# A decoder kernel's first cross attention: batches in turn, scores in three fp32r passes, splits and shares on POOL

## What is computed

```python
kv_rope = kv_c * cos[None] + _rotate_half(kv_c) * sin[None]
q_r = jnp.einsum('bshq,hqr->bhsr', q_big, W_qr)
k_r = jnp.einsum('bld,hdr->bhlr', kv_rope, W_kr)
scores = jnp.einsum('bhsr,bhlr->bhsl', q_r, k_r)
attn = jax.nn.softmax(scores, axis=-1)
ctx_c = jnp.einsum('bhsl,bld->bhsd', attn, kv_rope)
ctx_lat = jnp.einsum('bhsd,hkd->bshk', ctx_c, w_kc_kv)
out = ctx_lat.reshape(b, s, H * K) @ Wo.T
```

## Time and profile before

| | us |
|---|---|
| median of 3 runs (lowest, highest) | 1678.25 (1677.41, 1680.61) |
| the profiled execution: its time | 1680.23 |
| its span in the profile | 1678.4 |
| busy in it: PE, DVE | 1602.4, 991.4 |
| busy in it: ACT, POOL | 730.2, 508.6 |
| busy from 436 to 642 us (the stage): PE | 199.63 |
| DVE, ACT, POOL there | 146.00, 142.43, 5.47 |

### The profile page before, as it was taken

How to read it: one execution, slowest core, us unless ns; L and a number is a source line. 1 busy time by engine, 2 the same in 40 slices (tenths; PEclk the granted TensorE clock), 3 DMA queues, 4 the chain that set the end, 5 groups by cost and what they waited for, 6 DMA issues and landing times.

```text
span 1678.4 us, 24116 instructions
## 1 busy us (share of the span) xinstructions
PE 1602.4 (95%) x9668; PEld 1329.3 (79%) x9668; DVE 991.4 (59%) x1658; ACT 730.2 (44%) x1221; POOL 508.6 (30%) x335
## 2 busy tenths in 40 slices
PE   7999999999899999989999989999889999999998
PEld 6897667778688888867889987787677888878887
DVE  5555663455676675487758748244757455554555
ACT  2113664223577765666611146422635334353442
POOL 3875542520100002331117734111611432212321
PEclk9999999999999999999999999999999999999999
DMA  4110003134312004410001110110001111111111
GB/s 164 53 61 28 2 2 130 39 99 130 106 53 64 13 1 161 156 38 1 1 1 63 50 39 1 44 43 32 21 14 44 51 53 55 51 45 51 51 57 44
DMA packets 28578, 88.49 MB, mean 53 GB/s; under 512 B 4154, under 2 KB 4282, under 8 KB 28215
## 3 DMA queue, kind: packets, MB, share of 16 engines
q1 hardware_dynamic: 28468, 86.96, 15.6%
HBM read 85.11 MB, written 1.84 MB: 52 GB/s over the span
## 4 chain that ended last, share of the span: by engine, by line
PE 85%; DVE 8%; ACT 4%; issue 1%; POOL 0%; DMA 0%; ACTq 0%; DVEq 0%
PE PS L255 18%; PE PS L257 17%; PE PS L256 17%; PE PS L260 6%; PE PS L1026 5%; PE PS L1044 4%; PE PS L1376 3%; PE PS L932 3%; PE PS L1391 2%; PE PS L542 2%; PE PS L566 1%; PE PS L1623 1%; PE PS L1611 1%; PE PS L532 1%; DVE sm L1645 1%
## 5 line engine op out<-in xcount | busy, mean ns | idle before, releaser
L301 POOL TENSOR_TENSOR HL<-stg,HL 128x1024 fp32r<-128x1024 f32 (+2 forms) x111 | 244.0, 2201 | 824.2 <-ACT HL L296 803.8
L255 PE MATMUL PS<-XT,HL 128*128 128x448 f32 x608 | 225.3, 371 | 7.5 <-DVE XT L336 5.3
L257 PE MATMUL PS<-XT,HL 128*128 128x448 f32 x608 | 223.5, 368 | 0.0
L256 PE MATMUL PS<-XT,HL 128*128 128x448 f32 x608 | 223.5, 368 | 0.0
L296 ACT ACTIVATE HL<-stg 128x1024 fp32r<-128x1024 f32 (+2 forms) x111 | 104.2, 943 | 217.8 <-PE PS L257 202.5
L255 PE MATMUL PS<-HL,XT 128*128 128x512 f32 (+1 forms) x380 | 138.6, 365 | 3.7 <-DVE rs L316 1.6
L257 PE MATMUL PS<-HL,XT 128*128 128x512 f32 (+1 forms) x380 | 135.4, 356 | 0.0
L256 PE MATMUL PS<-HL,XT 128*128 128x512 f32 (+1 forms) x380 | 135.3, 356 | 0.0
L255 PEld LDWEIGHTS PS<-XT,HL 128*128 128x128 f32 x608 | 115.0, 189 | 19.1 <-DVE XT L336 6.0
L256 PEld LDWEIGHTS PS<-XT,HL 128*128 128x128 f32 x608 | 115.0, 189 | 9.7
L257 PEld LDWEIGHTS PS<-XT,HL 128*128 128x128 f32 x608 | 114.9, 189 | 9.8
(11 more groups left out here) (283 smaller groups left out, 3603.2 us busy)
## 6 DMA issues: line engine op xcount, KB each, us to landing
stg<-in_wst SPq DMA_DIRECT2D x87, 512.0 KB, 3.5
stg<-in_wst SPq DMA_DIRECT2D x16, 352.0 KB, 3.1
stg<-in_wst SPq DMA_DIRECT2D x16, 320.0 KB, 3.8
wsum<-in_wfc SPq DMA_DIRECT2D x8, 512.0 KB, 4.1
wsum<-in_wpj SPq DMA_DIRECT2D x8, 512.0 KB, 3.6
raw<-in_wfc SPq DMA_DIRECT2D x8, 512.0 KB, 6.7
stg<-in_wst SPq DMA_DIRECT2D x16, 256.0 KB, 2.6
raw<-in_wpj SPq DMA_DIRECT2D x7, 512.0 KB, 7.0
```

Source lines behind the costliest of these rows:

```text
L255: e.matmul(out, lh, rh, start=start, stop=False)
L256: e.matmul(out, lh, rl, start=False, stop=False)
L257: return e.matmul(out, ll, rh, start=False, stop=stop)
L301: e.tensor_tensor(slot(k)[:, 1, 0:n], stg[k % NSTG][:, 0:n], slot(k)[:, 0, 0:n].bitcast(F), A.subtract).then_inc(*done("pool_w", k))
```

## The change

- **Order.** Unit st takes batch `st // 8`: all 16 heads of a batch, then the next batch. `qx_at` and `pair_of` use slots 0 to 15 of `QO` (results go where the queries were); the freed slot and the room behind it hold the split queries.
- **Scores.** `mm3` on split queries (`qxh`, `qxl`: four heads of a batch, two buffers) and split keys (`kxh`, `kxl`: one batch, two buffers, padded by one column to 376).
- **POOL.** A new stage `pool_x` splits queries every second unit and the keys of the next batch every eighth, and scales the exponentials to shares, which DVE no longer does. The rest of "ox" 2 moves from the end of `pool_q` to step 3 of `pool_x`, behind the shares of unit 2.
- **Waits of PE.** It begins with the queries, the first split queries and the keys of batch 0, and waits for the last rotated values only ahead of the value products.
- **Hand-over.** Heads 0 to 7 are complete only at the end. `ox_hi` and `ox_lo` of the first four outputs are made in two parts: batches 0 to 5 in steps 52 to 59, batches 6 and 7 at the end of `act_x` and `dve_x` (there behind `threshold`). Tiles 0 to 4 of the first product need the first part alone.

```diff
+        kxh = [at(f"kxh{i}", [128, L + 1], R, (KVX + 6080, KVX)[i]) for i in range(2)]
...
         def qx_at(half, h):
-            s = 1 + 8 * (h // 8) + 4 * half
+            s = 8 * (h // 8) + 4 * half
             return QO[:, s:s + 4, h % 8, :]
...
             for b in range(NB):
                 rotate_rows(e, b)
-            for i in range(3):
...
+            last.then_inc(*done("pool_x", "pad"))
+            keys_parts(e, 0)
+            query_parts(e, 0)
+            for i in range(2):
                 rest_w(e, piece["ox", i][0])
...
+        def keys_parts(e, b):
+            e.wait_ge(*upon("dve_ctx", "k", b if b == 0 else NB - 1))
+            if b > 1:
+                e.wait_ge(*upon("pe_x", "sc", 8 * b - 9))
+            e.tensor_copy(kxh[b % 2][:, 0:L], kvT[:, b, :]).then_inc(*done("pool_x", "kh", b))
+            e.wait_ge(*upon("pool_x", "kh", b))
+            e.tensor_tensor(kxl[b % 2][:, 0:L], kvT[:, b, :], kxh[b % 2][:, 0:L].bitcast(F), A.subtract).then_inc(*done("pool_x", "k", b))
...
+        def query_parts(e, u):
+            i = u // 2 % 2
+            q = QO[:, 8 * (u // 4 % 2) + u // 8, 4 * i:4 * i + 4, :]
...
+            if u > 3:
+                e.wait_ge(*upon("pe_x", "sc", u - 3))
+            e.tensor_copy(qxh[i][:, :, :], q).then_inc(*done("pool_x", "qh", u))
+            e.wait_ge(*upon("pool_x", "qh", u))
+            e.tensor_tensor(qxl[i][:, :, :], q, qxh[i][:, :, :].bitcast(F), A.subtract).then_inc(*done("pool_x", "q", u))
+
+        def pool_x(e):
+            for st in range(UX + 1):
+                if st % 2 == 0 and st + 2 < UX:
+                    query_parts(e, st + 2)
+                if st % 8 == 4 and st // 8 + 1 < NB:
+                    keys_parts(e, st // 8 + 1)
+                if st:
+                    u = st - 1
+                    k = u % 4
+                    e.wait_ge(*upon("dve_x", "rx", u))
+                    for e_ in range(2):
+                        last = e.tensor_scalar(Sx[k][:, e_, :], Sx[k][:, e_, :], rx[:, k, e_:e_ + 1], None, A.mult)
+                    last.then_inc(*done("pool_x", "p", u))
+                if st == 3:
+                    rest_w(e, piece["ox", 2][0])
+
         def pe_x(e):
-            e.wait_ge(*upon("dve_q", "o", 7, 1))
-            e.wait_ge(*upon("act_q", "o", 7, 1))
-            e.wait_ge(*upon("dve_ctx", "k", 7))
-            e.wait_ge(*upon("pool_ctx", "k", 7))
             for st in range(UX + 4):
                 if st < UX:
-                    b, bank = st // 4 % 8, 2 * (st % 2)
-                    if st > 1:
+                    b, bank = st // 8, 2 * (st % 2)
+                    if st % 8 == 0:
+                        e.wait_ge(*upon("pool_x", "k", b))
+                    e.wait_ge(*upon("pool_x", "q", st // 2 * 2))
...
                     for e_ in range(2):
-                        last = e.matmul(PS[0:S, bank + e_, 0:L], QO[:, 1 + st // 4, 2 * (st % 4) + e_, :], kvT[:, b, :],
-                                        start=True, stop=True)
+                        i, j = st // 2 % 2, 2 * (st % 2) + e_
+                        last = mm3(e, PS[0:S, bank + e_, 0:L + 1], qxh[i][:, j, :], qxl[i][:, j, :], kxh[b % 2][:, :],
+                                   kxl[b % 2][:, :], True, True)
...
-                    e.wait_ge(*upon("dve_x", "p", u))
+                    e.wait_ge(*upon("pool_x", "p", u))
...
             value_hi(e, 1)
+            for c in range(4):
+                ox_hi(e, c, 1)
...
-                    e.wait_ge(*upon("dve_x", "rx", u))
-                    for e_ in range(2):
-                        last = e.tensor_scalar(Sx[k][:, e_, :], Sx[k][:, e_, :], rx[:, k, e_:e_ + 1], None, A.mult)
-                    last.then_inc(*done("dve_x", "p", u))
...
             threshold(e)
+            for c in range(4):
+                ox_lo(e, c, 1)
...
                 for t in range(NT):
+                    if c == 0 and t == 5:
+                        e.wait_ge(*upon("dve_ox", "lo", 0, 1))
```

More of the change, by code:

```diff
@@ L168, in build @@
         Sx = [at(f"Sx{i}", [S, 2, L], F, rSCR + i * 3008) for i in range(4)]
+        QOX, KVX = rQO + 16 * 8 * S * 4, rKV + 24288
+        qxh = [at(f"qxh{i}", [128, 4, S], R, QOX + i * 3584) for i in range(2)]
+        qxl = [at(f"qxl{i}", [128, 4, S], R, QOX + i * 3584 + 1792) for i in range(2)]
+        kxh = [at(f"kxh{i}", [128, L + 1], R, (KVX + 6080, KVX)[i]) for i in range(2)]
+        kxl = [at(f"kxl{i}", [128, L + 1], R, (KVX + 3008, KVX + 1504)[i]) for i in range(2)]
         PX = [at(f"PX{i}", [125, 2, 3, S], F, rSCR + 12032 + i * 2688) for i in range(2)]
@@ L1007, in pool_q @@
                 rotate_rows(e, b)
-            for i in range(3):
+            for i in range(2):
+                e.tensor_scalar(kxh[i][:, L:L + 1], C("ones")[:, 0:1], 0.0, None, A.mult)
+                last = e.tensor_scalar(kxl[i][:, L:L + 1], C("ones")[:, 0:1], 0.0, None, A.mult)
+            last.then_inc(*done("pool_x", "pad"))
+            keys_parts(e, 0)
+            query_parts(e, 0)
+            for i in range(2):
                 rest_w(e, piece["ox", i][0])
         UX = 64
+        def keys_parts(e, b):
[5 more added lines that the diff above has]
+            e.tensor_tensor(kxl[b % 2][:, 0:L], kvT[:, b, :], kxh[b % 2][:, 0:L].bitcast(F), A.subtract).then_inc(*done("pool_x", "k", b))
@@ new lines, in pair_of @@
+        def pair_of(u):
+            return QO[:, 8 * (u // 4 % 2) + u // 8, 2 * (u % 4):2 * (u % 4) + 2, :]
+        def query_parts(e, u):
+            i = u // 2 % 2
+            q = QO[:, 8 * (u // 4 % 2) + u // 8, 4 * i:4 * i + 4, :]
+            if u < 8 or u == 32:
+                e.wait_ge(*upon("dve_q", "o", u + 1 if u < 8 else 7, u // 32))
+                e.wait_ge(*upon("act_q", "o", u + 1 if u < 8 else 7, u // 32))
+            if u > 3:
[3 more added lines that the diff above has]
+            e.tensor_tensor(qxl[i][:, :, :], q, qxh[i][:, :, :].bitcast(F), A.subtract).then_inc(*done("pool_x", "q", u))
@@ L1042, in pe_x @@
                         e.wait_ge(*upon("dve_x", "o", u - 2))
+                    else:
+                        e.wait_ge(*upon("pool_ctx", "k", NB - 1))
                     for c in range(3):
-                        last = e.matmul(PS[:, 6 + u % 2, 0:2 * S], kvr[:, c, u // 4 % 8, :], PX[u % 2][:, :, c, :],
+                        last = e.matmul(PS[:, 6 + u % 2, 0:2 * S], kvr[:, c, u // 8, :], PX[u % 2][:, :, c, :],
                                         start=c == 0, stop=c == 2)
@@ L1112, in dve_x, with ox_batches, ox_src, ox_part @@
             threshold(e)
+            for c in range(4):
+                ox_lo(e, c, 1)
         OX = 16
         first_ox = piece["ox", 0][0]
[L1119 to L1126, removed]
+        def ox_batches(c, part):
+            return (0, NB) if c > 3 else (6 * part, 6 + 2 * part)
+        def ox_src(c, part):
+            b0, b1 = ox_batches(c, part)
+            return QO[:, 8 * (c // 8) + b0:8 * (c // 8) + b1, c % 8, :]
+        def ox_part(hl, c, part):
+            b0, b1 = ox_batches(c, part)
+            return XT[:, hl, c % 4, :].rearrange("p (b s) -> p b s", b=NB)[:, b0:b1, :]
+        def ox_hi(e, c, part=1):
+            e.wait_ge(*upon("dve_x", "o", 8 * ox_batches(c, part)[1] - 1))
             if c > 3:
                 e.wait_ge(*upon("pe_ox", "c", c - 4))
-            else:
+            elif part == 0:
                 e.wait_ge(*upon("act_mag", 15))
[L1131 to L1135, removed]
+            e.activation(ox_part(0, c, part), ox_src(c, part), ACT.Copy).then_inc(*done("act_ox", "hi", c, part))
+        def ox_lo(e, c, part=1):
+            e.wait_ge(*upon("act_ox", "hi", c, part))
+            e.tensor_tensor(ox_part(1, c, part), ox_src(c, part), ox_part(0, c, part).bitcast(F),
+                            A.subtract).then_inc(*done("dve_ox", "lo", c, part))
         def value_bank(j):
@@ L2368, in sync @@
             load(e, first_ox + 9)
[L2369 removed]
+            e.wait_ge(*upon("dve_ox", "lo", 7, 1))
             for j in range(7):
@@ L2404, in gpsimd @@
         def gpsimd(e):
-            for stage in (pool_proj0, pool_att0, pool_o0, pool_q, pool_ox, pool_ffn, pool_proj1, pool_att1, pool_o1, pool_q2, pool_att2,
+            for stage in (pool_proj0, pool_att0, pool_o0, pool_q, pool_x, pool_ox, pool_ffn, pool_proj1, pool_att1, pool_o1, pool_q2, pool_att2,
                           pool_o2, pool_moe):
```

18 lines of the change are left out of this document (10 added, 8 removed).

## The result

The changed kernel took 1715.7 us (median of 4 runs, 1711.91 to 1719.22), the kernel before 1679.43 beside it: ratio 1.0214, 95% interval 1.0199 to 1.0229. It is slower by 36 us, 2.1%; I had forecast 1672.6, faster. The profiled execution has a span of 1715.0 us against 1678.4.

A forecast was written before the change was run, and what follows sets the result against it. The prediction took PE to bound the stage, with POOL hidden: -13.6 us for the scores and +8.0 for a stall at the start gave -5.6, so 1672.6 us from a median of 1678.25, range 1662 to 1679.

The forecast's parts named there:

- the price of the scaling: POOL in the first cross attention: 0.55 us per scaling of 375 columns, from one-input rows.
- so POOL is hidden: POOL's work sums to 17.1 us per eight units, 2.1 a unit, against PE's 2.83.
- the upper bound: POOL's scalings and casts: at most the two-input price, 0.97 us per scaling.
- rival (b): POOL becomes the bound at two-input prices: 3.34 us a unit, 1702.8 us, slower; 10%.
- Scores: PE's scores in six fp32r matmuls at 0.172 us: unit 2.83, saving 13.6 us over 59 units.
- Rival (c): PE's weight loads are not hidden in the scores: +0.41 us a unit, 1710 us; 3%.
- The wait that takes its place: Stage start: late third weight rest delays the first wsum load, stalling ACT and PE; +8.0 us (+6 to +10.5).
- The gain of the earlier start: Stage start: batch order lets PE score before the last key rotation; -1.4 us if nothing stalled.
- Rival (a): The start does not stall, so PE gains 1.4 us there: 1663.3 us; 10%.
- The hand-over: Stage end: split output parts on DVE and ACT stay covered; 0 us, up to +2 if not.
- My terms: Whole kernel: -13.6 for the scores and +8.0 for the start, together -5.6 us.
- Moving the shares off DVE: DVE loses 0.74 us of work a unit, off the path: worth nothing.

The follow-up runs named there:

- e10: e2 with a second multiplication by 1.0 added to each POOL scaling; 1664.3 us.
- e2: The changed kernel with only the third weight rest ("ox" 2) moved back to the end of the queries' stage; 1703.2 us.
- e5: e2 with a constant as the scale in place of the reciprocal read from memory, so the division by the sums is left out; 1694.1 us.
- e3: The changed kernel with the scaling back on DVE and the third weight rest back in its early place; 1664.5 us.
- e4: e2 with one tensor_tensor of 112x750 and broadcast reciprocals on POOL in place of two tensor_scalar; 1664.8 us.
- e7: e4 with only the scores back to fp32 on unsplit queries and keys; 1681.2 us.
- e12: The changed kernel with only the second multiplication by 1.0 in the POOL scaling, third weight rest still late; 1674.0 us.
- e9: e2 with minimum and maximum with constants in place of the multiplication on POOL, division by the sums left out; 1665.3 us.

## Why the prediction was wrong

**The step that failed** is the price of the scaling, "I take 0.55", in the part on shares and splits, and with it "so POOL is hidden". The two rows of one-input operations behind it are both of instructions with two operations, a minimum and a maximum; the one-column row beside them, too, has two, both multiplications. I allowed for a scale read from memory; I did not note that the change's instruction has one operation where they all have two. That form takes 1.24 us, above even what I had set as the upper bound, the two-input price of 0.97. With it POOL needs, by the groups shown first, 16 x 1.24 for the shares, 4 x 1.69 for the queries and 1.42 for the keys, 28.0 us per eight units or 3.5 a unit, where PE needs 2.82. e10, with the second operation and nothing else changed against e2, brings it back to 0.596 us and the unit to 2.822.

**The rival (b) is what happened** (I had given it 10%): POOL became the bound. Its price was too low, though, and its reason another one: it took the two-input price as the dearest case and named the scale in memory, which e5 shows to be 0.08 us, not the single operation. Its figures were 3.34 us a unit and 1702.8; measured were 3.429 and 1715.7. Of the 12.9 us between, 5.1 are in the units (21.6 against 16.5), 2.0 in the start, 0.6 in the hand-over, and most of the rest is the scatter of the other stages. The low clock in mid-stage isn't among the causes, since POOL's work alone comes to the 3.5 us a unit.

**Scores: right.** Six matmuls at 0.172 were forecast to make the unit 2.83; it is 2.822 in e3, e4 and e10. e7 puts a price on that alone, 1681.2 against 1664.8, 16 us by medians and 13.6 by 58 x 0.235. The formula of the Trainium skill (TensorE: Matmul & The Clock Gate, Back-to-back issue gap), N/2.4 + 2.5 ns, gives 0.159 us for 376 columns, and by that estimate the unit would have been 2.75; it is 2.822, and the rows decided rightly. Rival (c), weight loads not hidden, is out: one score matmul follows the other at 0.17 us (three starts in a row at full clock are 657.47, 657.64 and 657.82).

**The wait that takes its place: right in mechanism, and in size once the scaling has the priced value.** e12 is the kernel I priced: start 26.05 against 19.02 before, +7.0 where +8.0 was forecast, and 1674.0 us where 1672.6 was forecast. Half of that 1.0 is the load, 4.0 us from its issue to the sum instead of 4.5. Behind unit 5's scores another 0.8 us is lost while the clock is still low (0.69 from 457 to 460 us). The gain of the earlier start, forecast as 1.4 if nothing stalled, is 19.02 - 17.41 = 1.6. In the change itself the start cost +10.0. Rival (a) fails with it.

**The hand-over: right.** From the scores of unit 63 to the first output product it is 11.1 us in every kernel where POOL doesn't bind, 11.14 before. DVE ended the four split parts near 680.2 us in the change, and no wait of PE for them shows.

**Sum.** My terms come to -5.6 and e12 measures 0.9966 of the kernel before, which is -5.7 us (-3.9 to -7.6 by its interval; the medians alone give -7.6). Term by term it is +7.0 and -12.8 against +8.0 and -13.6, so the agreement to 0.1 is in part two small errors that cancel. The large error was one price, 0.69 us too low in 128 instructions, and it turned some 6 us faster into 36 us slower.

## What to carry to other kernels

A price taken from another row must be of the same form of instruction: operation count, where the scalars come from, kinds of input. Moving the shares off DVE was counted as worth nothing in the prediction, and e3 and e4, level with each other, bear that out: it brought the risk and none of the gain. When a piece of work moves to an engine whose trace doesn't show it, work out from which price the engine binds, and treat a price with no row of its form as open in both directions, not as bounded by a dearer kind. And follow the queue of the transfer engine past every wait that the change moves: the rest of one weight piece held up sixteen loads that had nothing to do with it.

The best kernels here are the change with the third rest early and either form of cheap shares: e3, e4 and e10, 1664.3 to 1664.8 us, 0.99 of the kernel before. Among them the runs tell no difference; e10 is two small edits away from the change.

## What the runs showed that I had not expected

- POOL's tensor_scalar over 112 x 375 fp32 takes 1.24 us with one multiplication and 0.60 us with that and a second one by 1.0. With constants it is 1.17 for one operation and 0.50 for two (minimum and maximum). Why the form with one operation is slow no run here shows; width, alignment and the place of the scale are excluded.
- The scale's place in memory costs 0.08 us an instruction (e5 against e2). The 0.10 between e9 and e10 has that and another pair of operations in it.
- A multiplication of two inputs, one of them broadcast, on 750 columns takes 1.44 us, less than one of 375 columns twice in the slow form (2.49).
- DVE's scalings are slower where POOL casts queries at the same time: in e3 two of them take 1.04 us instead of 0.74.
- PE was busy for 87% of the stretch from 475 to 640 us (143.26 of 165), and its granted clock still fell in places. Around the wait of 2.20 us before 523.28 it was at full speed in the wait, at half while PE was working again, and back at 527:

```profile
522.00:523.00 1.00, 0.00 (x0) 0.00 (x0) 0.13 (x2) 0.00 (x0) 1.00 (x2) 1.00 0.06 16
524.00:525.00 1.00, 1.00 (x6) 0.96 (x6) 0.00 (x0) 0.20 (x1) 1.00 (x2) 0.50 0.00 0
527.00:528.00 1.00, 1.00 (x8) 1.00 (x8) 0.39 (x1) 0.00 (x0) 1.00 (x2) 1.00 0.00 0
```
